# Softmax chain woven into the first five unit ticks of the main phase, and edge weights spread by a TensorE product

## What is computed

```
edge_index = jnp.stack([src, dst])
h = jnp.maximum(_layernorm(x, axis=-1), 0.0)
x = x + _L0_gnn_ref(h, edge_attr_32, src, dst, ...)      # attention over the edges of one target
h = jnp.maximum(_layernorm(x, axis=-1), 0.0)
x = x + _L1_gnn_ref(h, src, dst, L1_gnn_fc_w, L1_gnn_fc_b)
...
# inside _L0_gnn_ref
logits = jax.nn.leaky_relu(w_feat @ a[:, 0])
seg_max = jax.ops.segment_max(logits, dst, num_segments=N_NODES)
ex = jnp.exp(logits - seg_max[dst])
seg_sum = jax.ops.segment_sum(ex, dst, num_segments=N_NODES)
att = ex / seg_sum[dst]
agg = jax.ops.segment_sum(att[:, None] * msg, dst, num_segments=N_NODES)
```

## Time and profile before

| What | Value |
|---|---|
| Median of 3 runs | 2545.1 us (2543.75 to 2546.36) |
| The profiled execution's own time | 2545.85 us |
| Its span in the trace | 2544.0 us |
| PE, DVE, ACT, POOL busy | 70%, 74%, 51%, 73% |

### The profile page before, as it was taken

The page is one execution under the profiler, slowest core; times in us unless marked ns, Lnnn a source line. Parts: engine busy times, 40 slices in busy tenths (PEclk is TensorE's granted clock), DMA queues, the critical chain, the costliest instruction groups (busy, mean ns, idle before and its releaser), DMA issues.

```text
span 2544.0 us, 26059 instructions
## 1 busy us (share of the span) xinstructions
PE 1793.5 (70%) x6414; PEld 865.8 (34%) x6414; DVE 1876.7 (74%) x3056; ACT 1300.2 (51%) x2694; POOL 1862.3 (73%) x1775
## 2 busy tenths in 40 slices
PE   3888877774997488877888787768888888850000
PEld 1433333322443243433444343333444344430000
DVE  6999987646888378987999788887999799960000
ACT  2676666532886265545666555545666566620000
POOL 5777777766777777746777677757777677777776
PEclk9999998886999699979999889989999899975555
DMA  2344433224776354433444356553444444440000
GB/s 65 101 121 132 118 109 84 69 73 125 229 241 215 97 167 135 138 125 104 115 129 125 107 163 200 176 185 111 126 117 126 115 146 129 134 133 22 23 21 20
DMA packets 240170, 309.75 MB, mean 122 GB/s; under 512 B 86875, under 2 KB 102389, under 8 KB 239896
## 3 DMA queue, kind: packets, MB, share of 16 engines
q1 hardware_dynamic: 183576, 281.76, 34.6%
q0 software_dynamic: 56448, 26.34, 5.8%
HBM read 188.24 MB, written 144.91 MB: 131 GB/s over the span
## 4 chain that ended last, share of the span: by engine, by line
POOL 25%; DVE 18%; PE 14%; issue 13%; ACT 5%; DMA 1%; DVEq 0%; SPq 0%; ACTq 0%; POOLq 0%
POOL mn_ring L515 17%; POOL out_dram L1883 8%; PE bank L1185 4%; DVE mn_total L1567 3%; DVE node_h L1391 3%; PE bank L1189 2%; PE bank L1194 2%; PE bank L1928 2%; PE bank L1179 2%; DVE node_h L1436 1%; PE bank L1199 1%; DVE mn_scaled L1583 1%; ACT node_square L1312 1%; ACT node_std L1296 1%; DVE mn_h L1646 1%
## 5 line engine op out<-in xcount | busy, mean ns | idle before, releaser
L515 POOL DMA_INDIRECT mn_ring<-slot_rows,addr_i x980 | 1041.7, 1063 | 389.3 <-issue 293.9
L1185 PE MATMUL bank<-node_x,center 128*128 128x512 f32 x492 | 250.1, 622 | 74.7 <-DVE node_h L1391 70.4
L515 POOL DMA_INDIRECT found<-node_table,look_i x196 | 211.8, 1081 | 84.3 <-issue 61.6
L1189 PE MATMUL bank<-node_square,mean 128*128 128x512 f32 x492 | 261.7, 614 | 4.7 <-ACT node_std L1291 4.0
L1194 PE MATMUL bank<-node_h,wconv 128*128 128x512 f32 x492 | 263.8, 619 | 0.3 <-DVE mn_sums L1701 0.3
L515 POOL DMA_INDIRECT xin<-in_x_dram,src_i x196 | 206.9, 1056 | 71.8 <-issue 59.5
L1312 ACT ACTIVATE node_square<-bank 128x512 f32<-128x512 f32 x246 | 145.9, 593 | 210.5 <-PE bank L1185 210.3
L515 POOL DMA_INDIRECT xin<-in_x_dram,dst_i x196 | 206.4, 1053 | 63.4 <-issue 59.5
L1306 ACT ACTIVATE node_act<-bank,bias 128x512 f32<-128x512 f32 x246 | 168.5, 685 | 154.1 <-PE bank L1194 153.7
L1883 POOL DMA_INDIRECT out_dram<-keep,scat_i x196 | 193.3, 986 | 62.5 <-issue 62.5
L1199 PE MATMUL bank<-node_act,wconv 128*128 128x512 f32 x442 | 230.2, 603 | 2.5 <-ACT node_act L1306 2.5
(11 more groups left out here) (334 smaller groups left out, 3808.2 us busy)
## 6 DMA issues: line engine op xcount, KB each, us to landing
mn_ring<-local SPq DMA_DIRECT2D x120, 256.0 KB, 4.1
out_dram<-node_rows SPq DMA_DIRECT2D x98, 256.0 KB
mn_rin<-res SPq DMA_DIRECT2D x96, 256.0 KB, 3.7
local<-node_rows SPq DMA_DIRECT2D x96, 256.0 KB
slot_rows<-keep SPq DMA_DIRECT2D x96, 256.0 KB, 2.0
mn_fcol<-f_rows SPq DMA_DIRECT2D x192, 128.0 KB, 4.1
res<-mn_x SPq DMA_DIRECT2D x72, 256.0 KB, 2.8
node_x_in<-in_x_dram SPq DMA_DIRECT2D x64, 256.0 KB
```

Source lines behind the costliest of these rows:

```text
L515: return eng.indirect_dma_start(out=dest, out_offset=None, in_=table, in_offset=bass.IndirectOffsetOnAxis(ap=index, axis=0), bounds_check= ...
L1185: pe.matmul(bank[i][:, :], C["center"][:, :], src, start=True, stop=True).then_inc(s["centered"][i], 1)
L1189: pe.matmul(bank[4][:, :], C["mean"][:, :], nd.square[:, i - 1, :], start=True, stop=True) \
```

## The change

The softmax phase goes. Its steps stand in the main phase, between the parts of the first five ticks (`OPENING = 5`, ticks 0 to 4), which now run ahead of stage A. `tail` is split into `body` and `tail`, so that softmax steps stand between the two. A's share of ticks is 0.75 for an iteration, not 1.0. A's weights come to PSUM by a product: `halves` (2 partitions) times the two rows of weights in `kv`, which one small DMA a group loads. POOL's lookups all stand in the main phase now, the first 40 unpaced. The DMA that broadcasts `same` moves to the front phase.

```diff
-LOOK_SOFT = 14
-LOOK_PACE = 8
+OPENING = 5
+LOOK_OPEN, LOOK_PACE = 40, 8
...
-SHARE = dict(A=1.0, B=0.72, C=1.0, D=0.72, E=1.0, F=1.05)
+SHARE = dict(A=0.75, B=0.72, C=1.0, D=0.72, E=1.0, F=1.05)
...
-    table, due, done = [], 0.0, 0
+    table, due, done = [], float(OPENING), OPENING
...
-            softmax_phase(K)
         main_phase(K)
...
                     if st == "A":
-                        v.wait_ge(s["fcol_in"][i % 2], 32 * fcol_uses(i))
-                        v.tensor_tensor(here, of_group(keep, g), fcol[:, i % 2, 0:w], ALU.mult).then_inc(s["gs"], 1)
+                        v.wait_ge(s["spread"], i + 1)
+                        v.tensor_tensor(here, of_group(keep, g), bank[6][:, 0:w], ALU.mult).then_inc(s["gs"], 1)
...
+                body(2)
+                down_rows("top")
+                tail(2)
+                down_join(top)
+                link(v.tensor_tensor(weight[0:KP, :], logit[0:KP, 0, :], top[0:KP, :], ALU.subtract))
+                mark["shifted"] = done[0]
+                v.wait_ge(s["weighed"], 1)
+                up("sum", sum_, C["k_same"], weight, sum_up)
+                body(3)
+                up_rows("sum", C["r_open"], C["crossf"], sum_up)
+                tail(3)
...
+                load(0)
+                load(1)
+                for t in range(OPENING):
+                    keep_local(t)
+                    tick(t)
+                fill_late(*order[0])
+                sp.wait_ge(s["late"], mark["att"])
+                for half in range(2):
+                    sp.dma_start(D["att"][half:half + 1, :].rearrange("o (c k) -> (o c) k", k=256),
+                                 share[64 * half:64 * half + ROWS, :]).then_inc(s["att_kept"], 16)
+                sp.wait_ge(s["att_kept"], 32)
                 fill_kv(*order[0])
                 fill_kv(*order[1])
...
-                    if j % LOOK_PACE == 0 and j > 0:
-                        gp.wait_ge(s["x"], j // LOOK_PACE)
+                    if j >= LOOK_OPEN and (j - LOOK_OPEN) % LOOK_PACE == 0:
+                        gp.wait_ge(s["x"], (j - LOOK_OPEN) // LOOK_PACE + 1)
...
+                def spread(i, w):
+                    pe.wait_ge(s["kv_in"][i % 2], 16 * (i // 2 + 1))
+                    if i >= 1:
+                        pe.wait_ge(s["gs"], i)
+                    pe.matmul(bank[6][:, 0:w], C["halves"][:, :], kv[:, i % 2, 0:w], start=True, stop=True) \
+                        .then_inc(s["spread"], 1)
...
+                for t in range(1, OPENING):
+                    first(t)
...
+                    second(t)
...
+                    third(t)
+
                 for i, (st, g) in enumerate(order):
+                    if st == "A" and g == 0:
+                        spread(i, w_of(g))
...
+                    if st == "A" and g < n - 1:
+                        spread(i + 1, w_of(g + 1))
...
+                for t in range(OPENING):
+                    if t == 3:
+                        act.wait_ge(s["late"], mark["shifted"])
+                        act.activation(weight[0:KP, :], weight[0:KP, :], ACT.Exp).then_inc(s["weighed"], 1)
+                    begin(t)
+                    rest(t)
```

More of the change, by code:

```diff
@@ L179, in build @@
                 v_d=sb("v_d", [P, 2], F32, early), v_e=sb("v_e", [F, 2], F32, early), c0=sb("c0", [P, 1], F32, early),
[L180 to L182 removed]
+                bmsg=sb("bmsg", [P, 1], F32, early), dst=sb("dst_i", [P, TILES], I32, early))
             with ExitStack() as ctx:
@@ L652, in _ @@
                 load_edges(0)
+                for h in range(2):
+                    sp.dma_start(C["same"][F * h:F * h + F, :], D["same"][h:h + 1, :].broadcast_to([F, HE])) \
+                        .then_inc(s["same_in"], 16)
                 load_units(0)
@@ L1401, in head, with body @@
                 .then_inc(s["cent1"], 1)
-    def tail(t):
+    def body(t):
         if 0 <= t - 2 < n:
@@ L1409, in tail @@
             v.tensor_tensor(nd.res[:, u % 2, :], nd.x2[:, u % 2, :], h, ALU.add).then_inc(s["res"], 1)
+    def tail(t):
         if 0 <= t - 3 < n:
@@ L1440, in tail @@
                 .then_inc(s["x2_rows"], 1)
-    return head, tail
+    return head, body, tail
 def main_phase(K):
@@ L1524, in gathers @@
             return 16 * sum(tiles(j % n) for j in range(n, i + 1) if j % R == i % R)
-        def fcol_uses(i):
-            return sum(1 for j in range(i + 1) if j % 2 == i % 2 and order[j][0] != "B")
         def h_uses(i, k):
@@ new lines, in up_join, with down @@
+                def up_join(out, gap_, op):
+                    answered()
+                    link(v.tensor_copy(col[0:KP, 0, 0:1], bank[7][0:KP, 128:129]))
+                    link(v.scalar_tensor_tensor(out[0:KP, :], gap_[0:KP, :], col[0:KP, 0, 0:1], out[0:KP, :],
+                                                op[0], op[1]))
+                    answered()
+                    link(v.tensor_copy(out[0:KP, 255:256], bank[6][0:KP, 0:1]))
+                def down(name, out, data):
+                    link(v.tensor_tensor(ends[0:KP, :], data[0:KP, :], C["k_last"][0:KP, :], ALU.mult))
+                    link(v.tensor_tensor_scan(out[0:KP, ::-1], C["k_nl"][0:KP, ::-1], ends[0:KP, ::-1], 0.0,
+                                              ALU.mult, ALU.add))
+                    mark[name] = done[0]
@@ new lines, in down_rows, with down_join @@
+                def down_rows(name):
+                    answered()
+                    link(v.tensor_tensor_scan(back_row[0:1, 0:KP][:, ::-1], C["r_nopen"][:, ::-1],
+                                              bank[7][0:1, 0:KP][:, ::-1], back_row[0:1, KP:KP + 1], ALU.mult, ALU.add))
+                    mark[name + " carry"] = done[0]
+                def down_join(out):
+                    answered()
+                    link(v.tensor_copy(col[0:KP, 0, 1:2], bank[7][0:KP, 128:129]))
+                    link(v.scalar_tensor_tensor(out[0:KP, :], C["k_nprod"][0:KP, :], col[0:KP, 0, 1:2], out[0:KP, :],
+                                                ALU.mult, ALU.add))
@@ L1702, in late @@
                     mark["so"] = done[0]
-                head, tail = node_vector(K, nd, v)
+                head, body, tail = node_vector(K, nd, v)
                 link(v.memset(pad[:, :, :], 0.0))
@@ L1737, in _ @@
                             head(t)
+                        body(t)
                         tail(t)
```

222 lines of the change are left out of this document (91 added, 131 removed).

## The result

The changed kernel takes 2551.99 us (median of 16 runs, 2547.5 to 2554.96) against 2544.31 us (16 runs, 2541.04 to 2547.34) before, a ratio of 1.0028 with a 95% interval of 1.0021 to 1.0034: 7.7 us slower. The profiled execution took 2552.51 us, 6.7 more than that of before.

A forecast was written before the change was run, and what follows sets the result against it. No single engine was named as the bound; POOL's lookups set B's start, with A 18 us in hand. `late()` +0.9, B +4.0 and C onward 0 gave +4.9 us, 2550.0 from 2545.1; range 2538 to 2561 for 8 times in 10.

The forecast's parts named there:

- the forecast case: The main forecast for the whole kernel: 2550.0 us, with 2545 to 2556 of its own; chance 0.45.
- Main opens: Start of the main phase: 578.4 instead of 601.4, as the softmax phase and its barrier's pause go.
- A's first scan: End of the opening: first scan at 623, with 2 us added for clock dips; ends 619 and 631.
- The product in A: `spread` between two ticks on PE: a ticked iteration behind a ticked one goes from 9.84 to 10.85 us.
- A's 24 intervals: Stage A, first to last scan: 213.1 us plus 3 for half clock, 216.1, against 214.2 before.
- From A's last scan to DVE's being free: End of stage A: 11.0 us as before, so DVE is ready at 850.1.
- The lookups: POOL's 188 lookups: last start 839.5, landed 841.9, 7.3 us earlier than 849.24, so no longer last.
- Stage B: 18 ticks where it had 17: one plain iteration becomes ticked, +4.0 us.
- Behind C: Stage C and all that follows: no change, 0 us.
- the hidden work: Rival: PE swallows `spread` and B's extra tick in idle gaps; -7.3 us, 2537.8; chance 0.18.
- the opening that crawls: Rival: clock stays at 0.50 until A is under way, first scan at 631; +10 more, 2560; chance 0.20.
- The third: Rival: `spread` is hidden in A but B's tick is paid; -7.3 + 4.0 = -3.3 us, 2541.8; chance 0.17.

## Why the prediction was right, step by step

The measured median lies 2.0 us above the predicted 2550.0, within the forecast case's own range of 2545 to 2556, and on the slower side of the bound of 0.2%, to which 0.43 had been given. The difference is less close: +4.9 us forecast, +7.7 measured, as the kernel before took 2544.31 us in this round and not 2545.1. The mechanism held, that A's own end takes over from the lookups at the seam and that B pays for its tick. The size of the first part, +3.2 us for +0.9, would have been off by 1.8 us more if main had not opened early, which was luck.

- **Main opens** at 576.6 and not 578.4. This is not shown to be an effect of the change: the first lookup behind the front phase lies between 577.59 and 579.25 in the four profiles of kernels with a softmax phase, and between 576.27 and 578.62 in the six without.
- **A's first scan**: predicted 623, measured 620.61. From the first lookup I had 43.7 us and it is 43.2. The clock rose near 594, earlier than I feared, and the two dips at 600 and 602 (products of 1.59 and 1.88 us) are within the 2 us that I had put in.
- **The product in A**: the mechanism was right, the size too small. I took the product as 1.04 us, from the earlier trace rows (and wrote 10.85 where 9.84 and 1.04 make 10.88); it costs 1.25. The row of L1881 to L1064 shows 1.06 us, and on either side of it the start of the next instruction comes 0.1 us later than with full-size neighbours (0.59 for 0.49, 0.96 for 0.86). The runs without the product, with the product alone and with it in the gap settle that this is what A's time went to.
- **A's 24 intervals**: predicted 216.1, measured 221.0. By kind: ten behind a ticked one take 110.9 us for 108.5; six behind a plain one 60.7 for 55.8; six plain ones 40.6 for 40.2; the two at the ends 8.8 for 8.6. That is 7.9 us more than the 213.1, of which I had 3 as clock. The middle term is that clock: three of the six took 9.4 as predicted, the first 11.8 and two 10.4. All six have products at half clock in them, and where these stand decides what they cost. In the two of 10.4 us it is the product in the tick's middle, for which ACT waits:

```profile
669.41 2.07 PE L1059 MATMUL bank<-node_square,mean 128*128 128x512 f32 x2 [2.56 <-ACT node_std L1161]
```

In the three of 9.4 us it is the tick's first products, which PE does while DVE is still busy with the plain iteration (2.97 of the 3 us from 703 on), and there they cost nothing (this tick's interval takes 9.37 us):

```profile
702.87 1.85 PE L1064 MATMUL bank<-node_h,wconv 128*128 128x512 f32 x2
...
704.52 1.91 PE L1059 MATMUL bank<-node_square,mean 128*128 128x512 f32 x2
```

- **From A's last scan to DVE's being free**: predicted 11.0, measured 10.9. So `late()` is at 852.47 and not 850.1: 2.4 early at the first scan (1.8 of it main's opening), 4.9 late in the intervals.
- **The lookups**: predicted last start 839.5, measured 836.95, and from the first lookup 259.5 us for 260.2. They no longer end last, as predicted. But the reason that I gave, no pause at a barrier and fewer ticked iterations, doesn't carry the number: the run with the two broadcasts has both and takes 268.9 us from its first lookup to its last, against 267.7 in the kernel before. Nor does the product alone, with 268.6. Only the four kernels that have both parts and a PSUM operand take 259.5 to 262.4 us, and why stays open; that the forecast met the number is luck. I bounded the price of the two SBUF operands by 1 and 10.5 us, and the profiles show about 2. The upper bound was a misreading of the earlier trace rows: the multiplication that starts at 702.90 has ended at 703.58, so the lookup of 1.42 us at 704.76 doesn't run beside it. The Trainium skill (SBUF — State Buffer, section "SBUF: two separate sides") says that a VectorE instruction with two SBUF inputs and a GpSimd instruction that reads SBUF lock one pair of ports against each other, and that the one that comes second is blocked until the first has ended. The direction agrees with the ten profiles (1.04 to 1.05 us for 1.00 to 1.01). The size doesn't look like a full block, as the multiplication takes 0.68 us.
- **Stage B**: predicted +4.0, measured +3.7. From `late()` to C's first gather, four profiles with 17 ticks in B have 302.8, 301.7, 305.0 and 303.6 us, six with 18 have 306.5, 306.2, 306.6, 305.9, 306.1 and 306.7. A difference of 3.0 on the mean, and the two runs that move that one tick, +3.3 and -3.0, put it down to the tick.
- **Behind C**: nothing, as predicted: 1391.1 us for 1392.0, and 1391.1 to 1391.8 in the other five profiles without a softmax phase. With that phase it is less steady: 1392.0 before, 1394.8 with `same` in the front, 1396.2 with the product alone and 1398.3 with the tick moved to B.

Of the rivals, the hidden work did not happen: a steady ticked iteration takes 11.09 us and not under 10. Nor did the opening that crawls. The third, with the product hidden and B's tick paid, is what the run with the product in the gap made true: `late()` at 842.76 for a forecast 841.9 (though DVE was ready only at 842.21 and not by 836, with one ticked interval of 13.86 us in a dip of the clock), and C's first gather at 1149.35, which is 2.6 us earlier than before, for a forecast 3.3. Its median shows no gain (the interval allows 2.5 us at most); whether the 2.6 us are lost again behind C or were particular to the profiled execution, the fastest of its 11 runs, stays open.

## What to carry to other kernels

A wait that goes is worth only what the next thing in line leaves: read both arrivals at the seam (here A's own end and POOL's last lookup) and add to each what the change gives it. A small instruction on an engine with 20% idle time costs its full length and a little more when it stands between two that run without a gap, and almost nothing when its data are made ready one step earlier and it is put where the engine waits. Work taken out of a steady rhythm can give back less than its length where TensorE idles for it: here one tick fewer saved 3.6 us and then lost 1.3 to the clock. And a tick moved to a stage's first iteration can cost what it costs elsewhere (3.3 us in B) or far more (9.0 us in A), so price it there.

## What the hardware showed that I had not expected

- A product of 512 columns over 2 partitions costs 1.25 us between full-size ones at full clock, more than its own 1.06 us.
- Two SBUF operands in DVE's multiplication lengthen the POOL lookups that run beside it from 1.00 to 1.04 or 1.05 us on the mean, about 2 us over the stage's 25 multiplications.
- The clock follows PE's use in a stretch: 4.85 us of products at the opening's start brought the full clock from about 594 to 582, and one plain iteration, with PE busy for 0.75 of 4 us, lost it for the next 7 us. It is not the only thing that loses it: in the changed kernel it fell at 703 with PE busy for 2.71 of the 3 us before, and why no run shows.
